# Two selective-scan stages: y banks doubled by half, decay factors in an SBUF ring of five, two states of each half without GpSimd

## The reference, cut to what matters

```python
x = einsum('ed,bld->bel', in_proj_w, ctx)            # 512 channels e, 512 positions l
u = silu(conv4(x) + conv_b)                          # per channel, 4 taps
dt_lo, Bm, Cm = split(einsum('ke,bel->bkl', x_proj_w, u))   # 16 states n
delta = softplus(dt_proj_w @ dt_lo + dt_proj_b)
A = -exp(A_log)
# for every position, over 16 states n:
dA = exp(delta * A[n])
state[n] = state[n] * dA + (delta * u) * Bm[n]
y += state[n] * Cm[n]
# after the scan
y = (y + D * u) * silu(layernorm(x_in))              # the gate
x_out = x_in + transpose(y)
```

## Time and profile before

| | us |
|---|---|
| median of three runs | 4288.59 |
| the profiled execution | 4288.35 |
| its span, first to last instruction | 4286.6 |
| VectorE busy over the span | 2941.3 |
| GpSimd busy over the span | 1535.4 |
| ScalarE busy over the span | 1765.4 |
| first stage, first scan starts | 87.42 |
| first stage, last product of VectorE ends | 577.73 |
| second stage, first scan starts | 3259.26 |
| second stage, last product of VectorE ends | 3749.55 |

### The profile page before, as it was taken

One profiled execution on the slowest core, in us unless ns is written; L12 is line 12 of the kernel. 1 busy time (PEld: TensorE's weight loads), 2 busy tenths in 40 slices (PEclk: granted clock), 3 DMA queues, 4 the chain that ended last, 5 costly groups with the idle time before them and its releaser, 6 DMA issues. The chain is left out here.

```text
span 4286.6 us, 46282 instructions
## 1 busy us (share of the span) xinstructions
PE 3607.8 (84%) x15168; PEld 1705.0 (40%) x15168; DVE 2941.3 (69%) x4121; ACT 1765.4 (41%) x2929; POOL 1535.4 (36%) x1070
## 2 busy tenths in 40 slices
PE   5788647999999999598999889775877777679898
PEld 2233214555555565342333344342332222234454
DVE  4888888577887773567887266447656888843663
ACT  4555322222222221243777253346645545321244
POOL 2999954112221120062000100014426999900122
PEclk8899878999999999797999989886988998989999
DMA  3455531133223212167663110010003544512420
GB/s 107 130 137 143 132 90 38 46 100 92 73 67 100 90 46 66 71 157 96 72 71 37 72 39 0 3 62 10 0 7 99 132 132 132 136 46 65 81 54 21
DMA packets 241368, 326.97 MB, mean 76 GB/s; under 512 B 40036, under 2 KB 141158, under 8 KB 240088
## 3 DMA queue, kind: packets, MB, share of 16 engines
q1 hardware_dynamic: 241160, 324.37, 30.9%
HBM read 276.33 MB, written 47.98 MB: 76 GB/s over the span
## 5 line engine op out<-in xcount | busy, mean ns | idle before, releaser
L521 POOL TENSOR_TENSOR m_dB<-m_du,m_BC 128x1024 f32<-128x1024 f32 x256 | 615.6, 2405 | 16.6 <-DVE m_du L553 16.6
L494 ACT ACTIVATE m_dA<-m_delta,m_a_neg 128x512 f32<-128x512 f32 x512 | 350.8, 690 | 486.5 <-DVE m_H_bank L588 419.7
L381 PE MATMUL m_y<-m_H,ident 128*128 128x512 f32 x512 | 294.2, 658 | 166.1 <-DVE m_H L599 166.0
L588 DVE TENSOR_TENSOR_SCAN m_H_bank<-m_dA,m_dB 128x512 f32<-128x512 f32 x256 | 315.0, 1230 | 127.9 <-POOL m_dB L521 103.6
L386 PE MATMUL m_y<-m_H,ident 128*128 128x512 f32 x512 | 293.4, 656 | 78.2 <-POOL m_H L506 78.2
L1631 DVE TENSOR_REDUCE a_core_minus_max<-a_core_a 128x1 f32<-128x512 f32 x512 | 317.1, 683 | 58.3 <-PE a_core_a L1457 58.3
L506 POOL TENSOR_TENSOR m_H<-m_H,m_BC 128x512 f32<-128x512 f32 x256 | 337.6, 1319 | 8.7 <-DVE m_H L593 7.9
L593 DVE TENSOR_TENSOR_SCAN m_H<-m_dA,m_dB 128x512 f32<-128x512 f32 x256 | 306.5, 1197 | 0.0
L1583 ACT ACTIVATE X<-a_core_s 128x512 f32<-128x512 f32 x512 | 264.5, 604 | 93.5 <-PE a_core_s L1457 93.4
L1023 POOL TENSOR_TENSOR ctxT<-ctxT,f_scales 128x1024 f32<-128x1024 f32 x48 | 107.0, 2228 | 532.3 <-DVE ctxT L848 532.3
L983 ACT ACTIVATE XN<-f_g,f_power_back 128x512 f32<-128x512 f32 x128 | 88.0, 687 | 402.9 <-PE f_g L920 402.9
(11 more groups left out here) (394 smaller groups left out, 7870.2 us busy)
## 6 DMA issues: line engine op xcount, KB each, us to landing
m_BC<-bc_rows SPq DMA_DIRECT2D x256, 512.0 KB, 4.8
XN<-in_L_ffn_w_dram SPq DMA_DIRECT2D x72, 256.0 KB, 2.7
ternary<-ctxT SPq DMA_DIRECT2D x96, 128.0 KB, 1.7
a_core_q<-a_q_parts SPq DMA_DIRECT2D x48, 256.0 KB, 12.8
a_core_k<-a_k_parts SPq DMA_DIRECT2D x48, 256.0 KB, 14.7
f_w_tern<-ternary SPq DMA_DIRECT2D x24, 512.0 KB, 6.4
f_core_q<-f_q_parts SPq DMA_DIRECT2D x24, 512.0 KB, 8.7
XN<-in_L_ffn_w_gate_dram SPq DMA_DIRECT2D x24, 256.0 KB, 2.7
```

The source lines that it names most:

```text
L381: pe.matmul(ps_y[:, 0, :], ident[:], HD[n % NH], start=False, stop=True, skip_group_check=True).then_inc(s_ad, 1)
L494: act.activation(dA[:, i % NA, :], delta[b % 2][:, e, :], ACT.Exp, scale=a_neg[:, e, k % N:k % N + 1]).then_inc(s_dA, 1)
L521: pool.tensor_tensor(dB[n % 2][:], du[b % 2][:, h * EH:(h + 1) * EH, :], BC[n % NS][:, 0:1, :].broadcast_to([P, EH, L]), ALU.mult).then_in ...
L588: dve.tensor_tensor_scan(ps_H[:], dA[:, 2 * n % NA, :], dB[n % 2][:, 0, :], 0.0, ALU.mult, ALU.add).then_inc(s_sc, 1)
```

## The change

- The decay ring `dA` moves from three banks of PSUM to `NA` = 5 rows of SBUF.
- `ps_y` gets two banks for each half (`y_of`), `ps_H` becomes two banks. `GATED` becomes 3 and `TURN`, `CONV` shift by a unit or two.
- `HD` and `HP` are rings of 4. dB gets `ND` = 4 buffers, of which two lie in `XN`; `positive` lies in `XN` as well.
- For the states k % 16 = 5 and 12 (`OWN`), the second scan writes to `ps_H`'s second bank and VectorE does the second product too.
- GpSimd's program is now dB(n), then product(n-2), without the products of own units.
- TensorE adds the second product two units late, not one.
- The gate is no longer normalised ahead of the scan. ScalarE computes Silu(scale * X + shift) for each batch at k = 10.

```diff
-        NH, NA = 3, 3
-        dB = [sb(f"dB{i}", [P, EH, L]) for i in range(2)]
+        NH, NA, ND = 4, 5, 4
+        dB = [sb(f"dB{i}", [P, EH, L])[:] for i in range(2)]
+        dB += [XN[:, 2 * TB + 2 * i:2 * TB + 2 * i + 2, :] for i in range(2)]
...
-        dA, ps_H = chip.ps(name + "_dA", [P, NA, L], F32, st), chip.ps(name + "_H_bank", [P, L], F32, st)
+        dA = sb("dA", [P, NA, L])
+        ps_y, ps_w = chip.ps(name + "_y", [P, 2, EH, L], F32, st), chip.ps(name + "_w", [P, 2, L], F32, st)
+        ps_H = chip.ps(name + "_H_bank", [P, 2, L], F32, st)
+        OWN = (5, 12)
...
-                        sp.wait_ge(s_hp, n - NS + 1)
+                        sp.wait_ge(s_hp, n - NS + 1 - owned(n - NS + 1))
+                        sp.wait_ge(s_ho, owned(n - NS + 1))
...
             def gates(b):
-                norm.wait(act)
-                for g in (0, 1) if b == 1 else (b,):
-                    act.activation(gate(g), gate(g), ACT.Silu).then_inc(s_z, 1)
+                for e in range(EB):
+                    t = b * TB + e
+                    act.activation(gate(b)[:, e, :], X[:, t, :], ACT.Silu, bias=norm.shift[:, t:t + 1],
+                                   scale=norm.rstd[:, t:t + 1]).then_inc(s_z, 1)
...
-            norm.odd_rows(act)
...
+                    if n >= ND:
+                        pool.wait_ge(s_sc, 2 * (n - ND + 1))
+                    pool.tensor_tensor(dB[n % ND][:], du[b % 2][:, h * EH:(h + 1) * EH, :],
+                                       BC[n % NS][:, 0:1, :].broadcast_to([P, EH, L]), ALU.mult).then_inc(s_dB, 1)
                     if n >= 2:
                         product(n - 2)
...
+            def first_scan(n):
+                dve.wait_ge(s_dB, n + 1)
+                dve.wait_ge(s_dA, 2 * n + 1)
+                if n:
+                    dve.wait_ge(s_hd, n)
+                dve.tensor_tensor_scan(ps_H[:, 0, :], dA[:, 2 * n % NA, :], dB[n % ND][:, 0, :], 0.0,
+                                       ALU.mult, ALU.add).then_inc(s_sc, 1)
...
+            def second_product(n):
+                dve.wait_ge(s_sc, 2 * n + 2)
+                if n >= NH:
+                    dve.wait_ge(s_ap, n - NH + 1)
+                dve.tensor_tensor(HP[n % NH], ps_H[:, 1, :], BC[n % NS][:, 1, :], ALU.mult).then_inc(s_ho, 1)
...
-            norm.even_rows(dve)
...
+                    first_scan(n)
+                    second_scan(n, ps_H[:, 1, :] if own(n) else HP[n % NH])
+                    first_product(n)
+                    if own(n):
+                        second_product(n)
```

More of the change, by code:

```diff
@@ L231, in stage_mamba @@
         xin = sb("xin", [P, EB, TAPS - 1 + L])
-        xdbl, positive = sb("xdbl", [W, L]), sb("positive", [P, EB, L])
+        xdbl, positive = sb("xdbl", [W, L]), XN[:, 3 * TB:4 * TB, :]
         u, delta, du = ([sb(f"{n}{i}", [P, EB, L]) for i in range(2)] for n in ("u", "delta", "du"))
-        NH, NA = 3, 3
-        dB = [sb(f"dB{i}", [P, EH, L]) for i in range(2)]
+        NH, NA, ND = 4, 5, 4
+        dB = [sb(f"dB{i}", [P, EH, L])[:] for i in range(2)]
+        dB += [XN[:, 2 * TB + 2 * i:2 * TB + 2 * i + 2, :] for i in range(2)]
         H = sb("H", [P, 2 * NH, L])
@@ L243, in stage_mamba, with y_of, own, owned @@
         norm = Norm(chip, name + "_norm", st)
-        ps_y, ps_w = chip.ps(name + "_y", [P, EH, L], F32, st), chip.ps(name + "_w", [P, 2, L], F32, st)
-        dA, ps_H = chip.ps(name + "_dA", [P, NA, L], F32, st), chip.ps(name + "_H_bank", [P, L], F32, st)
+        dA = sb("dA", [P, NA, L])
+        ps_y, ps_w = chip.ps(name + "_y", [P, 2, EH, L], F32, st), chip.ps(name + "_w", [P, 2, L], F32, st)
+        ps_H = chip.ps(name + "_H_bank", [P, 2, L], F32, st)
+        OWN = (5, 12)
+        def y_of(n):
+            return ps_y[:, n // N % 2]
+        def own(n):
+            return n % N in OWN
+        def owned(n):
+            return sum(own(i) for i in range(n))
         def gate(b):
-            return XN[:, b * TB:(b + 1) * TB, :]
+            return XN[:, b % 2 * TB:(b % 2 + 1) * TB, :]
         s_ld, s_wt, s_wc = sem("loaded"), sem("w_transposed"), sem("w_copied")
@@ L400, in _ @@
                     add_dve(n)
-            add_pool(B * NU - 1)
+            for n in range(B * NU - 2, B * NU):
+                add_pool(n)
             for item in ITEMS[-TB:]:
@@ L473, in _ @@
                 for k in range(NU):
+                    if k == SILU[0]:
+                        gates(b)
                     if b + 1 < B:
@@ L504, in product @@
             def product(n):
+                if own(n):
+                    return
                 pool.wait_ge(s_sc, 2 * n + 2)
@@ L549, in softplus @@
                 dve.wait_ge(s_relu, (b + 1) * EB)
-                dve.tensor_tensor(delta[b % 2][:], delta[b % 2][:], positive[:], ALU.add).then_inc(s_del, 1)
+                dve.tensor_tensor(delta[b % 2][:], delta[b % 2][:], positive, ALU.add).then_inc(s_del, 1)
                 dve.wait_ge(s_del, b + 1)
@@ L565, in add_y, with second_scan, first_product @@
                 dve.tensor_tensor(at, at, bank("turn", b, t), ALU.add).then_inc(s_add, 1)
+            def first_scan(n):
[5 more added lines that the diff above has]
+                                       ALU.mult, ALU.add).then_inc(s_sc, 1)
+            def second_scan(n, out):
+                dve.wait_ge(s_dA, 2 * n + 2)
+                if own(n):
+                    dve.wait_ge(s_ho, owned(n))
+                elif n >= NH:
+                    dve.wait_ge(s_ap, n - NH + 1)
+                dve.tensor_tensor_scan(out, dA[:, (2 * n + 1) % NA, :], dB[n % ND][:, 1, :], 0.0,
+                                       ALU.mult, ALU.add).then_inc(s_sc, 1)
+            def first_product(n):
+                dve.wait_ge(s_sc, 2 * n + 1)
+                dve.wait_ge(s_bc[n % NS], 16 * (n // NS + 1))
+                if n >= NH:
+                    dve.wait_ge(s_ad, n - NH + 1)
+                dve.tensor_tensor(HD[n % NH], ps_H[:, 0, :], BC[n % NS][:, 1, :], ALU.mult).then_inc(s_hd, 1)
+            def second_product(n):
+                dve.wait_ge(s_sc, 2 * n + 2)
+                if n >= NH:
+                    dve.wait_ge(s_ap, n - NH + 1)
+                dve.tensor_tensor(HP[n % NH], ps_H[:, 1, :], BC[n % NS][:, 1, :], ALU.mult).then_inc(s_ho, 1)
             log_error(0)
             norm.inverse(dve)
-            norm.even_rows(dve)
             softplus(0)
```

50 lines of the change are left out of this document (25 added, 25 removed).

## The result

The changed kernel takes 4740.72 us (median of 4 runs, 4735.88 to 4741.58), the kernel before 4289.51 beside it. The ratio is 1.1046 with an interval of 1.1032 to 1.1061: slower by 451 us, forecast were 463. The profiled execution took 4740.01 us, its span 4738.3.

The account below looks back on a forecast made before the run. GpSimd was taken to bound the kernel at 3.53 us a unit, VectorE 14% behind. Turns added 235.2 us a stage, the head took off 3.6: +463 over two stages, forecast 4751 us, range 4640 to 4890.

Parts of the forecast that it names:

- Scans and GpSimd take turns: Scan stages: with dA in SBUF, both scans alternate with GpSimd's dB and product; chance 0.88, +231.6 us a stage with head.
- The signs: Expected in the changed profile: scans 2.3 to 3.5 us, dB 3.4, product 2.3, dB starts 5.4 to 5.6 apart.
- Whoever waits gets its turn: VectorE and GpSimd at the ports: the waiting engine goes next even if the other has its next instruction ready.
- 5.51 a unit: Ordinary scan units: dB, product and two scans, 6.07 us in all, less four overlaps of 0.14; 112 a stage.
- Own units 4.37: Units where VectorE makes the second product: GpSimd drops 1.14 us, leaving 4.37; 16 a stage.
- Batch changes 12 each: At each batch change, add_error and VectorE's two-SBUF instructions already take turns, 12 us each; 38.5 kept a stage.
- Scan part 725.5: Scan part of one stage: 687.0 us of units plus 38.5, which is 235.2 more than 490.3.
- Head -3.6: Stage head: L172 and L178 go, so the softplus sum starts 3.6 us earlier; -3.6 a stage.
- TensorE's clock, the upper end: TensorE in a batch: its clock may fall, making its work 182 us, under 184; no cost taken, left to upper end.
- Rival 1: Scan units: scans don't contend and BC loads bound GpSimd at 4.2 us a unit, about 4440 us; chance 0.06.
- rival 2: Scan units: ports shared by width, scans cost half, 4.4 us a unit, 4518 us in all; chance 0.03.
- rival 3: Scan stages: no contention and BC loads landing in time make the kernel faster, 4232 us; chance 0.03.

Follow-up runs that it names:

- e1: Kernel before with only the three decay banks moved from PSUM to SBUF, ring of three kept: 4827.35 us, ratio 1.1256 to the kernel before.
- e2: Kernel before with only the second block's decays in SBUF, the first block's in two PSUM banks: 4596.58 us, ratio 1.0718.
- e4: Changed kernel with both GpSimd multiplications of a unit replaced by memsets, so its output isn't the reference's: 4209.87 us, one run.
- e3: Changed kernel with decays back in three PSUM banks, without doubled y banks, second H bank and own states: 4453.49 us, ratio 1.0384.
- e10: Changed kernel with decays in a PSUM ring of two, six BC buffers, own states 4 and 12: 4247.82 us, ratio 0.9900 to kernel before.

## Why the prediction was right, step by step

- *Scans and GpSimd take turns.* Shown by e1 (the tile's place alone: +540), e2 (the held scan is the one with two SBUF inputs) and e4 (beside GpSimd's memsets no holding up, beside its `add_error` 5.46 us for a scan). The Trainium skill, SBUF — State Buffer, section "Who interferes with whom", says that the contention is with a GpSimd instruction that reads SBUF and not with one that only writes; e4 agrees (1.23 and 1.20 beside a memset).
- *The signs.* Pitch 5.37, with 5.65 in the first batch, for 5.4 to 5.6; scans 2.2 to 2.4 for 2.3 to 3.5; dB 3.1 to 3.2 for 3.4; the product 2.0 for 2.3. The means came in just under the signs: they take in instructions that nothing holds, as the product in the first batch (1.27) and the scan behind an own unit (1.19).
- *One reading was too strong.* "Whoever waits gets its turn" holds for the four instructions of a unit, not for all: in the kernel before, the tensor_scalar of `log_error` (424.09, 5.27 us for 1.23) stood while GpSimd ran one instruction to its end and two more that began after it was let go. Nothing in the sum rested on it.
- *5.51 a unit.* It was 5.37 from the first batch change on, the overlap at each turn 0.17 to 0.18 rather than 0.14; and 5.65 in the first batch, for the semaphore. Against the sum's 5.51 the first batch's 23 units come to some 3 us a stage more and the settled ones to some 15 us less, so two errors cancel in part.
- *Own units 4.37.* In the changed kernel an own unit and the next take 5.76 and 3.96 (565.95 to 571.71 to 575.67), 9.72 for 2 x 5.37 less 1.02: 4.35 for the own one. Right.
- *Batch changes 12 each.* The eight units around the second and the third (from 394.22 and 575.67 on) last 55.5 us, 12.6 over 8 x 5.37; around the first it is 11.1.
- *Scan part 725.5.* 718.3, for the settled unit above all.
- *Head -3.6.* -3.4.
- *TensorE's clock, the upper end.* It stood at 0.73 and 0.81 in the two stretches, and VectorE and GpSimd wait for TensorE nowhere in the units of the first stage. At the end the last gating of y starts 3.0 us after VectorE's last product rather than 2.1 (805.33 against 802.34; before 579.86 against 577.73).
- *Rival 1.* It was not this kernel's case, but e3 shows that it was priced right (4440 forecast, 4453 measured) and hidden only by the greater loss: putting the decays back alone would have left 166 us on the table.
- *Rivals 2 and 3.* Out by e2 and by e1 with e3. The price of rival 2 leaves out the own units: 16 of them, each 1.14 shorter, make it 18 us a stage less, some 4480 rather than 4518. The gain that rival 3 named (4232) needed more than that the scans don't contend: e10, with everything mended, comes to 4248.
- *The rest of the change.* The sum had a price for the own states and the head, and nothing for the deeper rings, the y banks and the second H bank. e1, with none of all these, is slower than the changed kernel by 0.021 of the kernel before, 90 us: 32 own units at 1.02 each, 33; the head, 7; the shorter pattern (0.28 a unit, in 192 of the 256 units), 54. That is 94, worked out and not measured apart; the last term, if it is the rings', is the one that the sum had at nothing. The lower end of the range, 4640, lies 22 us above the bound that the working gives (4618), without a reason.

## What to carry to other kernels

Ask of each VectorE instruction how many of its inputs lie in SBUF while GpSimd runs instructions that read SBUF: a second one makes the two engines take turns for the whole length of both, and freeing a PSUM bank by moving such an input can cost more than any ring gains. Before an instruction is moved ahead of another on an in-order engine, count what now stands between the last reader of a buffer and the first user of its next load; a loss hidden behind a greater one will come out when that is mended. Work handed from GpSimd to VectorE pays only if it doesn't itself take a turn.

## What the runs showed of the hardware

- A turn leaves no gap: four instructions that last 6.07 us unhindered repeat every 5.37, an overlap of 0.17 at each of four handovers. A handover by semaphore between the same two instructions costs 0.08 instead (e1, e2), so the same work in another phase is 0.28 a unit longer.
- Who gets in next isn't always the one that waits longest: a two-input sum waited for one GpSimd instruction, the tensor_scalar of `log_error` in the kernel before until three were over (5.27 us), in the changed kernel for one (2.72 us at 399.38).
- A memset of GpSimd is not held by a scan with two SBUF inputs, but was by that tensor_scalar, which has one: 1.60 to 1.63 us for 0.52 at the three batch changes of e4's first stage (162.16 beside the tensor_scalar of 162.11).
- The time of a turn does not go with the size: the 16-element instruction of VectorE lasts 3.10 in the head of the changed kernel too (73.85), beside the `add_error` of 72.42.
- ScalarE's 128x512 exponential takes 0.72 into SBUF and 0.69 into PSUM.
